# VectorE's order in a two-layer graph attention kernel: the mask and the `ol` pass in front of the second layer's normalising pass

## The reference

```python
# layer 0
q, k, v = x @ Wq + bq, x @ Wk + bk, x @ Wv + bv          # 8 heads of 32
attn = softmax(where(adj == 0, -inf, q @ k.T / sqrt(32)))
y = (attn @ v) @ Wo + bo + x
x = (y - mean(y)) * rsqrt(var(y) + EPS) * gamma + beta
# layer 1
q, k, v = x @ Wq.T + bq, x @ Wk.T + bk, x @ Wv.T + bv
pros = softmax(where(adj == 0, -16384, q @ k.T))
z = v
for _ in range(4):
    z = 0.9 * pros @ z + 0.1 * v
y = x + z
out = (y - mean(y)) / sqrt(var(y) + EPS) * gamma + beta
```

## Time and profile before

| what | value |
|---|---|
| median of 3 runs | 841.31 us (840.86 to 842.0) |
| the profiled execution, its own time | 844.29 us |
| its span | 842.4 us |
| mean granted TensorE clock | 0.977 of full speed |
| busy: PE, DVE, ACT, POOL | 784.4, 716.7, 679.4, 554.3 us |

### The profile page before, as it was taken

One profiled execution on the slowest core, in us unless ns is written; L12 is line 12 of the kernel. 1 busy time (PEld: TensorE's weight loads), 2 busy tenths in 40 slices (PEclk: granted clock), 3 DMA queues, 4 the chain that ended last, 5 costly groups with the idle time before them and its releaser, 6 DMA issues. The chain is left out here.

```text
span 842.4 us, 33223 instructions
## 1 busy us (share of the span) xinstructions
PE 784.4 (93%) x11544; PEld 712.4 (85%) x11544; DVE 716.7 (85%) x3409; ACT 679.4 (81%) x2634; POOL 554.3 (66%) x421
## 2 busy tenths in 40 slices
PE   5789999999999999999999999999999999998883
PEld 4678999889889988988899889888988988897661
DVE  4578888899898888999988899898888999988655
ACT  3559988888898888888988888898888888989450
POOL 0236656667676776666777767676777676768566
PEclk9889999999999999999999999999999999999987
DMA  7101100010011111101111110011111101110001
GB/s 221 30 23 46 29 27 15 3 46 20 29 46 46 47 46 47 44 5 46 47 46 47 46 46 26 24 46 46 46 47 46 45 10 40 47 33 28 14 14 63
DMA packets 33219, 34.18 MB, mean 41 GB/s; under 512 B 2336, under 2 KB 28832, under 8 KB 33056
## 3 DMA queue, kind: packets, MB, share of 16 engines
q1 hardware_dynamic: 33056, 32.06, 12.8%
HBM read 23.67 MB, written 8.39 MB: 38 GB/s over the span
## 5 line engine op out<-in xcount | busy, mean ns | idle before, releaser
L590 ACT ACTIVATE ex<-sm,nmax 128x128 f32<-128x128 f32 x1024 | 398.0, 394 | 27.9 <-DVE nmax L738 27.6
L933 POOL TENSOR_TENSOR pr<-ex,rec 128x1024 f32<-128x1024 f32 x128 | 243.4, 1912 | 126.9 <-DVE rec L747 126.6
L738 DVE CUSTOM_DVE_ANT_0 sm<-psS,mask 128x128 f32<-128x128 f32 x1024 | 229.5, 284 | 6.8 <-PE psS L362 6.5
L590 ACT ACTIVATION_READ_ACCUMULATOR ex<-sm,nmax 128x1 f32 x1024 | 197.3, 193 | 0.0
L372 PE MATMUL psF<-ident,pr 128*128 128x128 f32 x1024 | 150.0, 280 | 5.5 <-issue 3.0
L599 ACT ACTIVATE pT<-psF 128x512 f32<-128x512 f32 x224 | 126.3, 593 | 30.6 <-PE psF L372 26.4
L372 PEld LDWEIGHTS psF<-ident,pr 128*128 128x128 f32 x1024 | 116.5, 143 | 17.4 <-issue 11.6
L313 PE MATMUL psF<-xh,w_hi 128*128 128x256 f32 x512 | 115.3, 307 | 14.2 <-DVE w_lo L677 7.5
L380 PE MATMUL psF<-pT,z 128*32 128x128 f32 x3072 | 110.5, 276 | 3.6 <-DVE z L840 2.7
L313 PE MATMUL psF<-xh,w_lo 128*128 128x256 f32 x512 | 104.2, 286 | 0.0
L313 PE MATMUL psF<-xl,w_hi 128*128 128x256 f32 x512 | 104.1, 285 | 0.0
(11 more groups left out here) (67 smaller groups left out, 1496.2 us busy)
## 6 DMA issues: line engine op xcount, KB each, us to landing
xt_in<-in_x_t SPq DMA_DIRECT2D x32, 256.0 KB, 3.5
x_in<-in_x SPq DMA_DIRECT2D x32, 256.0 KB, 3.1
out<-o_t SPq DMA_DIRECT2D x32, 256.0 KB, 2.2
adj_in<-in_adj SPq DMA_DIRECT2D x32, 128.0 KB, 2.9
w_raw<-in_w SPq DMA_DIRECT2D x7, 256.0 KB, 4.6
row<-in_rows SPq DMA_DIRECT2D x1, 768.0 KB, 6.5
ident<-in_ident SPq DMA_DIRECT2D x1, 64.0 KB, 3.8
col<-in_cols SPq DMA_DIRECT2D x1, 7.0 KB, 3.9
```

The lines of the kernel that those rows point to most:

```text
L590: e = nc.scalar.activation(ex[l][:, b, h, :], sm[l][:, b, h, :], ACT.Exp, scale=-1.0, bias=nmax[l][:, b, h:h + 1], accum_out=tot[l][:, b, ...
L738: last = nc.vector.tensor_tensor_reduce(sm[l][:, b, h, :], psS[:, o:o + N], mask[p.parity][:, b, :], -1.0, BIG, ALU.add, ALU.min, nmax[l][ ...
L933: nc.gpsimd.tensor_tensor(pr[l][:, b, :, :], ex[l][:, b, :, :], rec[l][:, b, :].unsqueeze(2).broadcast_to([128, H, N]), ALU.mult).then_inc ...
```

## The change

In VectorE's `step(t)`, `normalise(1, t - 6)` is issued after `make_mask(t)` and `save_ol(t - 1)` and no longer ahead of them. The instructions, their waits and every other engine's program are the same.

```diff
--- before.py
+++ after.py
@@ -907,9 +907,9 @@
                 mask_scores(1, 1, 1, t - 2)
                 mask_scores(1, 1, 0, t - 2)
                 reciprocals(1, 1, t - 3)
-                normalise(1, t - 6)
                 make_mask(t)
                 save_ol(t - 1)
+                normalise(1, t - 6)
                 if t.is_(1):
                     save_fold(0)
                     save_fold(1)
```

## The result

| | before | changed |
|---|---|---|
| median of 4 runs each | 841.65 us | 830.81 us (827.81 to 831.24) |
| the profiled execution | 844.29 us, span 842.4 | 827.81 us, span 825.9 |
| one step of the loop, `ol` to `ol` | 24.28 us | 23.80 us |

The ratio is 0.9856, 95% interval 0.9821 to 0.9891. In a later batch the changed kernel gave 828.74 us against 843.13, ratio 0.9836 (0.9814 to 0.9858). The forecast of 828.0 against 841.31 is a ratio of 0.9842. As a time, the first median lies 2.8 us above the forecast and just inside its own range (825.5 to 831.0).

The account below looks back on a forecast made before the run. DVE, held behind POOL's `pr`, was taken to close the loop; 26 × 0.47 = 12.2 plus 1.1 at the last `ol` saves 13.3 us, profiled 844.29 to 831.0, less 3.0 for the median: 828.0, own range 825.5 to 831.0 (72%).

Parts of the forecast that it names:

- What bounds: Loop over the pairs: the second normalising half stands 1.6 us behind POOL's `pr`, making DVE late down to `hT`.
- these 0.89: Loop steps with the normalising pass: 0.89 us lost per step, 24.28 against 23.39, all by DVE being late.
- Mask and `ol` beside `pr`: DVE behind the reciprocal: mask starts 0.09 us ahead of `pr`, `ol` 0.13 behind its start, neither held.
- slower rival: At the mask: POOL starts `pr` first and holds the mask; `sm` 0.45 us later, 853.0 us; chance 7%.
- The pass: Normalising pass behind `ol`: ends 0.47 us behind `pr`; `sm` then starts 2.34 behind the start of `pr`, before 2.82.
- The step: Loop step with all three passes: falls by 0.47 us, from 24.28 to 23.81; 12.2 us over 26 steps.
- What is late next: PE's wait for `ol` goes; it waits about 0.4 us for `hT` at `turn_hop(0,0)`; ACT and POOL follow DVE.
- The last `ol`: Step of the last `ol` at 776 us: saves between 0.1 and 1.27 us, taken as 1.1.
- the forecast 13.3: Whole kernel: total saving in us, 12.2 from the 26 steps plus 1.1 from the last `ol`.
- The 0.89 rival: Loop step: all 0.89 us come back, period falls to PE's 23.39; 24.2 us saved, 817.1 us; chance 4%.
- half: Loop step: `sm` starts as late as the aggregate did, or another wait appears; 7.6 us saved, 833.7 us; chance 12%.
- no change: Loop: something else, equally late, closes it, so the time stays at 841.3 us; chance 5%.

## Why the prediction was right

- **What bounds.** A DVE instruction that stands behind POOL's `pr`, in a loop that DVE closes at `hT`. Shown from three sides: with nothing held the step falls to PE's 23.39; with `ol` early but `sm` late it falls by 0.12 of these 0.89; with `sm` early and the pass behind it, it is only 0.07 below that of the changed kernel.
- **Mask and `ol` beside `pr`.** Expected at −0.09 and +0.13 us from its start; measured −0.09 and +0.13. The slower rival did not happen, but the order of 0.09 us on which it hung is real: once behind, the mask took 1.31 us. Its price (853.0) was not measured, as no order had the mask directly behind the reciprocal and yet behind the start of `pr`.
- **What the earlier trace rows also say.** The section of rows calls them both halves issued with POOL at work, but the first of them starts at 814.26 and `pr` at 814.33: it was 0.07 us ahead by the records and was held all the same. So a small lead was no safe sign, and for a lead of 0.09 the forecast stood on the earlier trace rows alone. These showed the very order that was to be built, and it came out.
- **The pass.** Expected to end 0.47 behind `pr`, measured 0.47. `sm` at 2.34, measured 2.35.
- **The step.** 23.81 forecast, 23.80 measured. The sum over the 26 steps, 12.2, came out as 0.69 + 11.89 = 12.6; the first step gave a little more, since PE there still ran as in the short steps.
- **What is late next.** PE lost 0.38 us at `turn_hop(0,0)`, where 0.4 was forecast. ACT and POOL followed DVE; `z0s` waits 2.03 instead of 2.51.
- **The last `ol`.** 1.1 taken out of 0.1 to 1.27; measured 1.02, with `z` as the late one, as worked out.
- **What the sum did not hold.** 0.41 us of start and 2.49 us of tail in the profiled pair, the latter under a different granted clock. The medians, 10.8 us apart in the first comparison and 14.4 in the second, lie on both sides of the forecast 13.3; single executions of one kernel differ by 3 to 6 us (the kernel before: 839.83 to 845.87 in 23 runs).
- **The 0.89 rival** was rightly held unlikely for this order, but its premise, that DVE's lateness could be covered, is what another order brings about, the pass in front of the reciprocal. The "half" and "no change" cases have nothing left for them.

The Trainium skill, page "SBUF — State Buffer", section "SBUF: two separate sides", has it that the first to start keeps the shared pair for its whole instruction. The orders tried here agree for the mask, 0.30 us when first and 1.31 when second, and for the first normalising half, 0.37 us when 0.16 ahead of `pr` and 1.38 when behind its start. The late pass shown below, 0.08 us ahead and held, does not fit if the recorded starts are taken for the order.

## What to carry to other kernels

Where a pass can be held by another engine's instruction, ask for each order what is issued before that instruction, what can run beside it, and what is left in the open behind it; here the last was the cost. The best place found for such a pass was in front of what releases the other engine: putting it ahead of the reciprocal gave 0.89 us a step, filling the hold with other work gave 0.48. That holds where the other engine's result can come later without harm, as `pr` could here by 0.65 us. A few steps of the same loop without the pass, here at its start, tell both the floor and whether the fillers are held, before anything is built.

## What the runs showed of the hardware that was not expected

- A recorded start slightly ahead of POOL's is not enough in every case. In the changed kernel a first half that started 0.08 us ahead of `pr` was held to its end, and `pr` was not delayed:

```profile
797.52 2.12 DVE L825 TENSOR_SCALAR o_t<-y,mv,rstd 128x256 f32<-128x256 f32 x1
...
797.60 1.90 POOL L933 TENSOR_TENSOR pr<-ex,rec 128x1024 f32<-128x1024 f32 x1 [2.30 <-DVE rec L747]
```

  The same pass was held at leads of 0.06 to 0.08 in the nine traces that issue it behind that reciprocal, and was free at 0.16. The mask was free at 0.085 to 0.089 in every step. Whether the limit lies in this narrow gap, or the mask (constants as scalars, integer input) needs less lead than the half (which reads `mv` and `rstd`), no run tells.
- POOL's next instruction gets in before the DVE instruction behind a held one. With two POOL instructions back to back, POOL's second started 0.11 us ahead of the next DVE instruction, and two DVE instructions were each held once (1.13 and 1.12 us), so splitting the POOL instruction does not free the second.
- `pr` is slightly longer when a free pass starts just ahead of it: 1.96 us with the mask 0.09 ahead, 1.95 to 1.96 with the first half 0.16 ahead, and 1.90 with neither in front. With the mask 0.16 ahead (the kernel with the pass in front of the reciprocal) it is 1.90 as well.
- `sm`, which waits over a semaphore for the mask directly in front of it, started 0.41 us behind the mask, 0.13 behind its recorded end; an independent `ol` started 0.20 behind it, 0.08 ahead of the end. Behind a held mask the distance from the end was 0.13 again (125.17 + 1.31 to 126.61). The scores were not the cause: behind another order `sm` could start 1.42 us behind `pr`, here it started at 2.70. With an independent pass between mask and `sm` the delay is gone.
